# A graph-network kernel: batched one-hot comparisons, an fp32 first product, and a new order of the side work

## The reference

```python
# block 1: GCN with batch norm and GELU
xw  = x @ W.T
deg = segment_sum(1, dst);  dinv = deg ** -0.5
h   = segment_sum(dinv[src] * dinv[dst] * xw[src], dst) + b
h   = gelu(batch_norm(h, gamma, beta)) + x
x   = layernorm(x + h)
# block 2: two relational layers, relu between them
w   = einsum('rb,bio->rio', att, basis)          # 2 relations, 30 bases of 512x512
msg = sigmoid(x[dst] @ gate_w[r]) * x[dst] @ w[r]   # r = type of the edge
agg = segment_sum(msg, src) + x @ root + bias
out = layernorm(x + layer2(relu(layer1(x))))
```

## Time and profile before

| what | value |
|---|---|
| median of 3 runs | 326.71 us (326.15 to 327.0) |
| the profiled execution | 326.88 us, its span 325.0 us |
| outside the span | 1.9 us |
| PE busy | 283.5 us (87%) |
| DVE busy | 175.3 us (54%) |
| ACT busy | 135.3 us (42%) |
| mean granted TensorE clock | 0.942 of full speed |
| DMA | 73.68 MB, mean 227 GB/s |

### The profile page before, as it was taken

The page is one execution under the profiler, slowest core; times in us unless marked ns, Lnnn a source line. Parts: engine busy times, 40 slices in busy tenths (PEclk is TensorE's granted clock), DMA queues, the critical chain, the costliest instruction groups (busy, mean ns, idle before and its releaser), DMA issues.

```text
span 325.0 us, 4963 instructions
## 1 busy us (share of the span) xinstructions
PE 283.5 (87%) x1711; PEld 193.4 (60%) x1711; DVE 175.3 (54%) x538; ACT 135.3 (42%) x265; POOL 36.5 (11%) x71
## 2 busy tenths in 40 slices
PE   1768899885969999568999999999997999999991
PEld 1653455432336786424767656647795777787771
DVE  3878787999967847686310132233325125433333
ACT  4596868899701368647243114111313142100000
POOL 1001000000002900551000000000003600010000
PEclk9987999998695999779999999999998999999997
DMA  6974869599997999739998677975001400001112
GB/s 175 335 327 158 336 257 356 207 388 416 352 385 282 314 354 418 313 103 367 382 381 318 260 292 303 418 294 246 2 0 32 132 0 0 2 0 33 33 34 63
DMA packets 12759, 73.68 MB, mean 227 GB/s; under 512 B 1952, under 2 KB 2195, under 8 KB 4540
## 3 DMA queue, kind: packets, MB, share of 16 engines
q1 hardware_dynamic: 11282, 70.82, 57.4%
q0 software_dynamic: 1104, 2.36, 2.8%
q10 hardware_dynamic: 346, 0.17, 0.3%
HBM read 72.05 MB, written 1.28 MB: 226 GB/s over the span
## 4 chain that ended last, share of the span: by engine, by line
PE 61%; DVE 22%; issue 7%; DMA 4%; DVEq 2%; ACT 1%; POOL 1%; ACTq 0%; POOLq 0%
PE psW L495 13%; PE psM L476 10%; PE psM L477 9%; PE psM L478 9%; PE psM L717 6%; PE psM L737 6%; DVE oh_key L1047 4%; DMA basis_ring<-in_L_gnn_basis_dram 3%; PE psM L623 3%; DVE B L1038 2%; PE psE L570 2%; DVEq L1032 2%; DVE w L1027 1%; DVE x_sum L1170 1%; DVE AT L1103 1%
## 5 line engine op out<-in xcount | busy, mean ns | idle before, releaser
L495 PE MATMUL psW<-basis_ring,S 128*32 128x512 f32 x512 | 68.2, 651 | 3.2 <-DMA basis_ring<-in_L_gnn_basis_dram 3.1
L1217 DVE SCALAR_TENSOR_TENSOR zg<-psM,gate,zg 125x512 fp32r<-125x512 f32 x20 | 15.0, 751 | 59.5 <-ACT zg L891 59.5
L1047 DVE TENSOR_SCALAR oh_key<-iota_f,key 128x160 f16<-128x160 f16 x162 | 36.0, 262 | 2.6 <-PE psE L570 1.4
L785 ACT ACTIVATE oh_diff<-iota_f,edgeT 128x128 f16<-128x128 f16 x108 | 34.1, 389 | 3.4 <-DVEq L964 3.4
L495 PEld LDWEIGHTS psW<-basis_ring,S 128*32 128x32 f32 x512 | 13.9, 115 | 32.5 <-issue 26.4
L476 PE MATMUL psM<-w,hlT 128*125 128x512 f32 x80 | 33.1, 414 | 0.1
L891 ACT ACTIVATE zg<-psM,gate 125x512 fp32r<-125x512 f32 x20 | 13.8, 688 | 46.1 <-PE psM L478 45.7
L477 PE MATMUL psM<-w,hlT 128*125 128x512 f32 x80 | 32.3, 404 | 0.0
L478 PE MATMUL psM<-w,hlT 128*125 128x512 f32 x80 | 32.1, 402 | 0.0
L570 PEld LDWEIGHTS psE<-oh_key,oh_src 128*125 128x125 f16 x162 | 16.0, 150 | 25.2 <-issue 19.2
L570 PE MATMUL psE<-oh_key,oh_src 128*125 128x160 f16 x162 | 21.3, 261 | 10.2 <-issue 6.6
(11 more groups left out here) (159 smaller groups left out, 430.5 us busy)
## 6 DMA issues: line engine op xcount, KB each, us to landing
basis_ring<-in_L_gnn_basis_dram SPq DMA_DIRECT2D x64, 1024.0 KB, 7.1
root_raw<-in_L_gnn_root_dram POOLq DMA_DIRECT2D x32, 64.0 KB, 3.6
xs<-in_x_dram SPq DMA_DIRECT2D x1, 1120.0 KB
out_dram<-xs SPq DMA_DIRECT2D x5, 224.0 KB
w_raw<-in_L_gnn_W_dram SPq DMA_DIRECT2D x1, 1024.0 KB, 10.9
bias_b<-in_L_gnn_bias_dram POOLq DMA_DIRECT2D x1, 250.0 KB, 3.8
xs<-in_x_dram SPq DMA_DIRECT2D x1, 130.0 KB
out_dram<-xs SPq DMA_DIRECT2D x5, 26.0 KB
```

Of the source, the lines that this page charges most:

```text
L495: m = nc.tensor.matmul(psW[32 * j:32 * j + 32, cc % 2, :], S[:, cc % 2, cc // CH, q].rearrange("p k r -> p (k r)"), ring[:, n % RING, j, : ...
L785: nc.scalar.activation(oh_diff[:, g % 3, j * P:(j + 1) * P], iota_f[:, 0:P], ACT.Abs, bias=edgeT[:, 0, g * G + j:g * G + j + 1], scale=-1. ...
L1047: v.tensor_scalar(oh_key[:, t % OH, :], iota_f[:, 0:KEYS], key[:, t:t + 1], None, ALU.is_equal) \
```

## The change

1. **Comparisons in one instruction for a group.** A place and a key are stored twice next to each other in fp16 (`place_pairs`, `key_pairs`), and `one_hots` compares a broadcast counter with a broadcast pair by one `tensor_tensor`: 6 x 160 = 960 elements for the keys, 4 x 126 = 504 for the places. The ring of `oh_key` goes from 12 to 18 tiles. `key_ready` counts groups.
2. **Place one-hots.** `GA` goes from 4 to 2: ACT makes two of the six in a group, DVE four.
3. **Register reads.** `window_at` stands in front of waits, behind a comparison; both windows of a group are added one after the other.
4. **First product in fp32.** No high and low parts: ACT alone copies the turned matrices (`turned_out`), `turned_low` is gone, and each of the 20 steps is one fp32 product. `W` is loaded in the basis's order by 4 DMAs instead of 1, so that the vectors are needed in one order alone. The steps are spread over groups 5 to 26 (`xw_upto(2 * (g - 3) // 3)`) with five left behind the loop.
5. **Basis parts.** In the count stage 16 instead of 24; later `basis_upto` calls have other numbers. Merges, high and low parts move accordingly.
6. **Diagonal.** The identity is put into `B` by five ACT copies at the start, and taken out of `BB` by five DVE subtractions before layer 1; `AT` needs one addition for each chunk. The diagonals for `dinv_b` are made by POOL, broadcast behind the first aggregation product, and copied by ACT.

```diff
-OH = 12
-GA = 4
+OH = 3 * G
+GA = 2
+PLACES = PC + PC % 2
...
-            use(name, "dve")
+            use(name, "act")
...
-        FIRST_XW = 4
+        PARTS_IN = 15
-        TURNED_LOW_AT = {1: (0, 1), 2: (2, 3), 3: (4, 5), 4: (6, 7), 5: (8,)}
+        TURNED_AT = {1: (0, 1), 2: (2, 3), 3: (4, 5), 4: (6, 7), 5: (8,)}
-        FIRST_AT = {8: 0, 17: 1}
-        HIGH_AT = {13: 0, 22: 1}
-        MERGE_AT = {11: 0, 20: 1}
-        LOW_AT = {14: 0, 23: 1}
+        MERGE_AT = {16: 0}
+        LOW_AT = {19: 0}
...  SP
-            sp.dma_start(w0_raw[:], W0.rearrange("(c p) o -> p c o", p=P)).then_inc(w0_in, 16)
+            for j in range(JB):
+                sp.dma_start(w0_raw[32 * j:32 * j + 32], W0.rearrange("(k c j) o -> j k c o", k=2 * KB, c=KC)[j]) \
+                    .then_inc(w0_in, 16)
...  POOL, behind dinv_p
+            for c in range(NC):
+                nc.gpsimd.tensor_scalar(diag[:, c, :], ident[0:PC, 0:PC], dinv_p[:, c:c + 1], None, ALU.mult) \
+                    .then_inc(diag_ready, 1)
...  PE
-                mm3(bank(("xw", c))[0:PC, :], xT_hi[:, k, n], xT_lo[:, k, n], w0T_hi[:, k], w0T_lo[:, k],
-                    k == 0, k == KC - 1)
+                last[0] = nc.tensor.matmul(bank(("xw", c))[0:PC, :], xT[:, k, n], w0T[:, k], start=(k == 0), stop=(k == KC - 1))
...
+                pe.wait_ge(key_ready, g + 1)
-                    pe.wait_ge(key_ready, t + 1)
-                if FIRST_XW <= g < FIRST_XW + NC * KC // 2:
-                    xw_part(2 * (g - FIRST_XW))
-                    xw_part(2 * (g - FIRST_XW) + 1)
-                basis_upto(9 * g // 10)
+                xw_upto(2 * (g - 3) // 3)
+                basis_upto(min(2 * g // 3 - 2, PARTS_IN))
...
+            xw_upto(NC * KC)
-            basis_upto(24)
-            basis_upto(25)
-            basis_upto(26)
+            basis_upto(17)
+            basis_upto(19)
...
-                basis_upto((28, 30, 31, 32)[f])
-            basis_upto(33)
+                basis_upto((21, 23, 25, 27)[f])
...  behind the transposes of hf
+            basis_upto(29)
-                basis_upto((35, 36, 37)[c])
+                basis_upto((31, 33, 35)[c])
-                    basis_upto(39 + KC * h + f)
+                    basis_upto((37, 37, 39, 39, 41, 41, 43, 43)[KC * h + f])
-                            basis_upto(47 + 7 * (R * c + r) // 5)
+                            basis_upto((45, 47, 47, 49, 51, 51, 53, 55, 55, 57)[R * c + r])
-                    basis_upto(min(60 + KC * h + f, 2 * CH * SUB - 1))
+                    basis_upto((57, 59, 59, 61, 61, 63, 63, 63)[KC * h + f])
...  ACT
+            for c in range(NC):
+                nc.scalar.activation(B[:, c, 0, c * PC:(c + 1) * PC], ident[0:PC, 0:PC], ACT.Copy).then_inc(b_zero, 1)
...
-                if f == 2:
+                if f == 1:
+                    w_high(1)
+                if f == KC:
                     w_high(2)
                     w_first(3)
...  DVE
+            def one_hots(out, pairs, first, n, width):
+
+                pair = iota_f[:, 0:width].rearrange("p (k i) -> p k i", i=2)
+                shape = [P, n, width // 2, 2]
+                return v.tensor_tensor(out, pair.unsqueeze(1).broadcast_to(shape),
+                                       pairs[:, first:first + n].unsqueeze(2).broadcast_to(shape), ALU.is_equal)
+
+            for g in range(NG):
+                if g >= 3:
+                    dve.wait_ge(adj_used, G * (g - 2))
+                src = oh_src[:, g % 3].rearrange("p (t e) -> p t e", t=G)[:, GA:, 0:PLACES]
+                one_hots(src.rearrange("p t (k i) -> p t k i", i=2), place_pairs, g * G + GA, G - GA, PLACES)
+                at = [window_at(2 * (g - 2))] if g >= 2 else []
+                one_hots(oh_key[:, g * G % OH:g * G % OH + G].rearrange("p t (k i) -> p t k i", i=2), key_pairs, g * G, G, KEYS) \
                     .then_inc(key_ready, 1)
+                if g >= 2:
+                    at.append(window_at(2 * (g - 2) + 1))
...
+                for i, w in enumerate(range(2 * (g - 2), 2 * (g - 1)) if g >= 2 else ()):
+                    add_window(w, at[i])
...
             for c in range(NC):
-                link(v.tensor_tensor(AT[:, c], B[:, c, 0, 0:N2], B[:, c, 1, 0:N2], ALU.add))
-                d = AT[:, c, c * PC:(c + 1) * PC]
-                v.tensor_tensor(d, d.bitcast(F32), ident[0:PC, 0:PC], ALU.add).then_inc(at_ready, 1)
-            w_merge(2)
+                v.tensor_tensor(AT[:, c], B[:, c, 0, 0:N2], B[:, c, 1, 0:N2], ALU.add).then_inc(at_ready, 1)
...  behind z
+            w_merge(1)
+            dve.wait_ge(dinv_b_ready, 2)
...  batch norm
-                if f == 2:
-                    w_low(2)
+                if f == 1:
+                    w_low(1)
+                if f == 2:
+                    w_merge(2)
...  layer norm
-                if c == 1:
-                    w_merge(3)
...  behind the first three x1_lo
-            w_low(3)
+            w_low(2)
+            w_merge(3)
...
+            w_low(3)
             w_merge(4)
             w_low(4)
...
+            for d in range(NC):
+                own_edge = BB[:, d * (R * NC + 1) * PC:(d * (R * NC + 1) + 1) * PC]
+                last = v.tensor_tensor(own_edge, own_edge.bitcast(F32), ident[0:PC, 0:PC], ALU.subtract)
+            link(last)
             z_parts(0)
```

More of the change, by code:

```diff
@@ L255, in gnn_block @@
         use("deg", "dve")
-        for h in range(2):
-            use(("dinv", h), "dve")
         NBB = -(-NC * R * NC // 4)
@@ L264, in gnn_block @@
                 use(("agg0", f, h), "dve")
+                if (f, h) == (0, 0):
+                    for i in range(2):
+                        use(("dinv", i), "act")
                 for b in BB_STEPS[2 * f + h]:
@@ L335, in own, with turned_from @@
             return BG * q - bases(q).start
-        def turned_parts(i):
+        def turned_from(i):
             what, c = turned[i]
@@ L559, in _, with xw_upto @@
             done()
+            steps_done = [0]
+            def xw_upto(n):
+                for i in range(steps_done[0], n):
+                    xw_part(i)
+                steps_done[0] = max(steps_done[0], n)
             for i in range(FIRST_TURNS):
@@ L604, in _ @@
             done()
-            basis_upto(25)
-            pe.wait_ge(diag_ready, 1)
-            for h, (c0, c1) in enumerate(((0, 4), (4, NC))):
-                wait_free(pe, ("dinv", h))
-                for c in range(c0, c1):
-                    last[0] = nc.tensor.matmul(bank(("dinv", h))[:, (c - c0) * PC:(c - c0 + 1) * PC], ones_f[0:PC, :],
-                                               diag[:, c, :], start=True, stop=True)
-                done()
-            basis_upto(26)
+            basis_upto(17)
+            basis_upto(19)
             for f in range(KC):
@@ L626, in _ @@
                     done()
+                    if (f, h) == (0, 0):
+                        pe.wait_ge(diag_ready, NC)
+                        for i, (c0, c1) in enumerate(((0, 4), (4, NC))):
+                            wait_free(pe, ("dinv", i))
+                            for c in range(c0, c1):
+                                last[0] = nc.tensor.matmul(bank(("dinv", i))[:, (c - c0) * PC:(c - c0 + 1) * PC],
+                                                           ones_f[0:PC, :], diag[:, c, :], start=True, stop=True)
+                            done()
                     for b in BB_STEPS[2 * f + h]:
@@ L824, in _ @@
                 nc.scalar.activation(z[:, 0, c, :], xw[:, c, :], ACT.Copy, scale=dinv_p[:, c:c + 1]).then_inc(z_hi, 1)
+            for i, (c0, c1) in enumerate(((0, 4), (4, NC))):
+                wait_full(act, ("dinv", i))
+                link(nc.scalar.activation(dinv_b[:, c0 * PC:c1 * PC], bank(("dinv", i))[:, 0:(c1 - c0) * PC], ACT.Copy))
+                act.sem_inc(free_act, 1)
+                act.sem_inc(dinv_b_ready, 1)
             act.wait_ge(z_ready, NC)
+            w_first(2)
             for f in range(KC + 1):
@@ L1112, in _ @@
             for c in range(NC):
-                last = v.tensor_scalar(diag[:, c, :], ident[0:PC, 0:PC], dinv_p[:, c:c + 1], None, ALU.mult)
-            last.then_inc(diag_ready, 1)
-            for c in range(NC):
                 dve.wait_ge(z_hi, c + 1)
```

142 lines of the change are left out of this document (63 added, 79 removed).

## The result

| | before | after |
|---|---|---|
| median (lowest to highest) of 15 runs | 326.84 us (326.15 to 329.15) | 325.36 us (320.08 to 327.92) |
| span of the profiled execution | 325.0 us | 326.1 us |
| DVE busy | 175.3 us | 159.6 us |

The ratio is 0.9872, with an interval of 0.9828 to 0.9915: the kernel became 1.3% faster, about 4 us, where 18 had been forecast. This ratio rests on the 4 of the 15 executions of after that lie within 1.5% of its fastest; the profiled one (327.92 us) is the slowest of the 15, so that the trace of after ends later than its ratio says, and the medians of all executions are only 0.5% apart. What follows uses that trace for places and durations, ratios for verdicts, and gives medians beside them where after is one side.

A forecast was written before the change was run, and what follows sets the result against it. Three engines and the basis loads were taken as near their limits in turn in the count stage. From 326.9 us, -24.6 (group 26 earlier) + 0.8 + 1.0 + 1.5 + 1.8 + 1.85 = -17.65 gave 309.2, median 309; range 299 to 321.

The forecast's parts named there:

- the pair moved ahead takes the reserve: +1.0 (between 0 and 5.6, two loads): Batch norm: four pairs stay in the aggregation, where loads were at their limit; the pair moved ahead costs +1.0 us.
- They just fit: Count stage: 12 basis loads at 373 GB/s take 33.7 us, as much as 21 groups of PE (34.2).
- the loads set the pace: Rival: PE waits for pairs from group 14 on and in the aggregation, 3 us in each; 315 us, 14%.
- Two windows at 0.33 one behind the other, with the same overlap, cost 0.60; the register reads [...] cost nothing: DVE, count stage: two windows take 0.60 us of a 1.69 us group; reads are hidden while long comparisons run.
- a fall of the clock in the count stage: Sign of failure: the clock falls to 1.2 GHz in the count stage because PE waits for whole groups.
- The kind of the comparisons: DVE, count stage: batched comparisons cost 0.67 us for 960 elements and 0.42 for 504, middles between two ends.
- A step of the fp32 product: PE, first product: a step costs 0.86 us where three terms cost 0.69, 3.4 us dearer over 20 steps.
- The wait in `root1` for `w_merge(3)`: After root1's first tile: the pair waits for w_merge(3), +1.8 us; one more pair in aggregation h adds +1.85.
- "+1.5" for the last GELU: Batch norm: ACT makes high part 2 and first half 3 in front of the last GELU, +1.5 us.
- The rival of the batched handoff: Count stage: DVE and PE alternate instead of overlapping, a group costs 3.3 us; 343 us, 4%.
- The first rival: DVE, count stage: two-tensor comparisons run one element at a time, 12 us more on DVE; 320 us, 14%.
- the third: Rival, count stage: PE is the limit, comparisons near the lower ends, DVE keeps ahead; 303 us at best, 8%.

The follow-up runs named there:

- 10: Kernel of 3 (new kernel, old placement) with each basis load from the fifth on cut to half; ratio 0.9636 against the kernel before.
- 3: New kernel with basis parts, merges, halves and low parts back at the old placement (24 parts in the count stage); ratio 0.9631 against before.
- 5: Kernel before with only the new placement of basis parts, merges, high and low parts (16 in the count stage); ratio 1.0264 against before.
- 1: New kernel with each basis load from the fifth part on cut to half; ratio 0.9651 against the kernel before.
- 2: Kernel before with each basis load from the fifth part on cut to half; ratio 1.0001 against the uncut kernel before.
- 4: New kernel with the first window between the two comparisons and both register reads behind the first comparison; ratio 0.9921 against before.
- 14: New kernel with one pair instead of two in front of the first aggregation, each later one moved back a place; ratio 0.9822 against before.
- 13: New kernel with only a quarter of root1 loaded and used for all four blocks; ratio 0.9732 against before.
- run 12: Kernel of 1 (half loads) with windows apart, one behind each comparison, and one register read behind each comparison; ratio 0.9461 against before.
- 16: Kernel of 14 with full loads, windows apart and one register read behind each comparison; ratio 0.9622 against before.
- 8: Kernel of 3 with the first product as one fp32r term, low parts left out; ratio 0.9633 against before.
- 15: Kernel of 3 with full loads, windows apart and one register read behind each comparison; ratio 0.9597 against before.

## Why the prediction was wrong, step by step

**The first step that failed: "the pair moved ahead takes the reserve: +1.0 (between 0 and 5.6, two loads)".** "They just fit" was right for the count stage itself, where PE waits for no load. But the prediction compared totals of loads and of PE for that stage alone, and made no such sum for the next one. The ring holds four parts, so what the queue doesn't move while the ring is full is lost. After moved eight parts out of a stage in which their loads cost nothing (10 against 3) to the one behind it, in which PE uses four parts in 5.3 us and eight more during the first aggregation. Its size is shown from three sides: putting the placement back gives 2.4% (after against 3, 7.9 us by the ratios, 10.2 by the medians), putting it into the kernel before costs 2.6% (5, 8.6 us), and halving the loads brings back 2.2% (after against 1, 7.2 us, 9.5 by the medians) while it does nothing for before (2). Most of it lies between `hf` and `root1`: 46.1 to 49.5 us with the new placement and full loads (4, 5 and after), 39.6 to 40.6 us in all kernels with the old one or with half loads. In that stretch the forecast had 39.7 + 2.5. What was lost there is 6 to 10 us: against half loads PE is idle for 5.6 to 5.8 us more, and in the trace of after it also works 3.7 us longer at a lower clock. The rival "the loads set the pace" named this mechanism, but priced it at 6 us with a gain of 24.6 in front of it, and from group 14 on; what was seen begins behind the count stage.

Why the queue is late there is shown only in part. Neither the burst (14) nor `root1` (13) alone is the cause, since the stretch stays at 45.5 and 44.3 us without them. By the windows the queue moves 16.4 MB in the stretch of after (332 GB/s in 49.5 us) and 16.8 in that of 14 (368 in 45.5), where before has 12.0 (302 in 39.7). As an estimate from these rows, 16.4 MB in 40 us would take 410 GB/s, about what the queue had in run 3 with little beside it (409, from 20 to 50 us). That the demand of the stretch as a whole is too high fits this; 13 and 14 together were not tried.

**The second: "Two windows at 0.33 one behind the other, with the same overlap, cost 0.60; the register reads [...] cost nothing".** They cost 0.70 and 0.36. The overlap was taken from comparisons that don't wait for each other, while the second window waits for the first; in run 12, each window between two comparisons, they cost 0.24 and 0.23, and with the reads one behind each comparison the group takes 1.65. Against the sum, windows and reads were 0.46 dearer and the comparisons 0.18 cheaper: the group took 1.97 instead of 1.69, 21 x 0.28 = 5.9 us. Putting the windows apart gave 6.4 us at `AT` (12 against 1) and 6.8 (16 against 14). The 5.9 us are half of the 11.8 us by which the count stage was longer than in the sum. That the rest of the difference, about 6 us, is made up of a later start (group 5 at 29.15 where 25.4 was predicted and run 1 has 26.20, with the edges read at 8.88 instead of 6.39 as in run 1; 2.3 us between these two runs at `AT`), 1.3 us of waiting in front of the merge, and two pairs that ran in part at 1.2 GHz (granted clock 0.60 of full speed from 50.0 to 53.7 and from 60 to 64 us), is read from the trace and was not tested:

```profile
50.61 3.08 PE psW L500 x16
...
53.78 0.75 DVE w_both L1030
...
60.31 3.29 PE psW L500 x16
```

Other pairs of the chain take 1.85. The prediction named a fall of the clock in the count stage as a thing that would make it wrong; here it fell after PE had waited 1.4 and 3.1 us for windows, and cost 2.7 us over two pairs, a part of which is hidden.

**Right were these steps.** The kind of the comparisons: their pitch is 0.57 for the keys and 0.34 for the places, below the 0.67 and 0.42 of the sum and far below one element at a time. The Trainium skill, "VectorE: DVE Perf Modes", section "The perf-mode tier table", with two elements a cycle, gave 0.57 and 0.33 as an estimate: trace and rule agree. The middle that the sum took instead was 0.18 a group too dear.

A step of the fp32 product cost 0.90 against 0.86 (29.75, `PE psM L548 x2`), and PE's product is not the limit (8). From the first product of group 26 to `hf` 20.1 us passed, where before had 18.9: +1.1 against +0.8; the degree products took 2.82 against 3.0. The wait in `root1` for `w_merge(3)` is in the chain, and from `root1` to the end after takes 3.0 us longer than before, where 1.8 + 1.85 had been counted; the old placement gives them back (3). "+1.5" for the last GELU behind ACT's weights was too much: run 1 has the same order, and its last GELU starts 22.9 us behind `hf` (118.99), where before has 22.0; from there to `root1` it takes 17.1 us against 17.6. This term and the 0 for the layer norm come to +0.4. The rival of the batched handoff would have made the kernel slower: it decides from 2.5 us a group on, and from group 5 (29.15) to group 26 (78.27) a group took 2.34 on PE, merges and tests included. PE and DVE do alternate in places (PE waits 8.8 us for windows), but not throughout. The first rival falls with the pitch of 0.57, the third with the total; run 8, on the old placement, speaks against it too.

**The sum again**, in the trace of after: -12.8 up to group 26 (predicted -24.6), +1.1 (+0.8), +9.8 (+2.5), +3.0 (+3.65) is +1.1, the difference of the spans. By the ratio after is 5 us better than this trace. The 9.8 and the start of the count stage are the terms that differ from trace to trace: with the same placement, run 4 has 6.4 more than before in the stretch.

**Left open.** Why after spreads over 8 us (15 executions) where 3 and 16 spread over 1.3 (four each) wasn't tested. Two things are seen to differ between the traces of after and of run 4 with the same placement: the granted clock between `hf` and `root1` (0.90 and 0.96) and the longest link (14.9 and 13.3 us). Nor is it settled why the windows apart bring 6.8 us with 16 parts in the count stage and 2.2 with 24 (15), although loads alone (10) and PE's product alone (8) bring nothing there. In 15 the waits on the ring rise from 10.5 to 13.1 us, which fits a stage with three limits close together. The old placement with windows apart and half loads would show it and was not run.

## What to carry to other kernels

When side work is moved, ask in which stage its transfers are free: a ring of n slots carries over n loads and no more, so idle time of the queue in a stage that another engine paces can't be used later. Price a change of the instruction stream and a change of the order of loads apart, and try them apart, since here the one was worth 12 us and the other cost 7 to 10 of them. Two short instructions of which one waits for the other belong between long independent ones (1.97 to 1.65 us a group, reads included), and of two register reads each wants a comparison of its own in front.

## What the hardware showed that was not expected

- A burst of loads into an empty ring lands late: a part of 1 MB landed 4.5 to 14.9 us after its issue between 80 and 130 us (median 9.3), since four were in the queue, at 283 to 315 GB/s for much of the time (100 to 115 us).
- The queue's rate at a full share isn't one number: 409 GB/s in run 3 with little beside it, 326 in after while 1 MB of 64 KB pieces came over another queue, 371 with a quarter of those.
- A DMA share of 0.97 is no sign that loads cost anything: halving them in the kernel before gave a ratio of 1.0001.
- Two additions of 160 columns, the second waiting for the first, cost 0.70 us together, and 0.24 each when an independent instruction stands between them.
- A comparison of pairs in fp16 has a pitch of 0.34 us for 504 elements and 0.57 for 960; in the loop 0.11 and 0.25 are added with a register read behind each.
- Two reads behind one comparison leave 0.48 to 0.54 us of idle time in front of a window (4 and 6), one behind each 0.16 to 0.19 (after and 12).
- The same placement and loads took 46.1 us from `hf` to `root1` in one trace and 49.5 in another, of which 3.2 are PE's work at a granted clock of 0.96 and 0.90.
